# Attention and mixture-of-experts layer on one core: the input brought a second time, already turned, and normalised in that layout on GpSimd

## The reference, cut to what matters

```
x = L0_attn_x                                        # (8, 1024, 256), float32
xn = layernorm(x)                                    # (x - mean) / sqrt(var + 1e-5) over the 256 columns
q, k, v = xn @ Wq.T, xn @ Wk.T, xn @ Wv.T            # 16 heads of 16 columns
a = causal_softmax(q k^T / 4) v                      # for each of 8 sequences and 16 heads
x = x + layernorm(a @ Wo.T)
x = x + layernorm(top-2-of-8 expert FFN of layernorm(x))   # 8192 tokens, 256 -> 2 x 512 -> 256
```

## Time and profile before

| | |
|---|---|
| runs | 1973.35 us median of 3 (1972.48 to 1975.88) |
| the profiled execution | 1972.61 us, of which the profile's span is 1970.9 us |
| start | up to about 96 us (first exponentials) |
| attention | about 96 to 1150 us, a quad every 29.43 to 35.44 us |
| expert FFN and end | about 1150 to 1971 us |
| busy over the span | PE 1843.2 us (94%), DVE 1541.8 (78%), ACT 1310.9 (67%), POOL 865.1 (44%) |
| the four transposes of a pair, pairs 6 to 31 | 104 of 273 ns, line 1441 |
| normalisation on ACT, copy out of ps_w on ACT | 2 x 595 ns and 592 ns a pair |

### The profile page before, as it was taken

One profiled execution on the slowest core, in us unless ns is written; L12 is line 12 of the kernel. 1 busy time (PEld: TensorE's weight loads), 2 busy tenths in 40 slices (PEclk: granted clock), 3 DMA queues, 4 the chain that ended last, 5 costly groups with the idle time before them and its releaser, 6 DMA issues.

```text
span 1970.9 us, 75491 instructions
## 1 busy us (share of the span) xinstructions
PE 1843.2 (94%) x26766; PEld 1280.2 (65%) x26767; DVE 1541.8 (78%) x5221; ACT 1310.9 (67%) x3291; POOL 865.1 (44%) x1247
## 2 busy tenths in 40 slices
PE   6899999999999999999999899999999999999980
PEld 3245555555545555455444369999999999999970
DVE  3888888888888888888888658778777777777767
ACT  5177788888888888888787766554445445554437
POOL 4333343445545555555454744544333333333336
PEclk9799999999999999999999999999999999999995
DMA  7744657475655656465557569889899999998848
GB/s 203 219 120 131 196 171 213 150 208 183 184 172 170 189 154 203 137 192 158 167 163 234 169 206 279 240 250 265 252 260 264 257 264 261 264 262 245 239 119 342
DMA packets 255062, 411.72 MB, mean 209 GB/s; under 512 B 34480, under 2 KB 191920, under 8 KB 247600
## 3 DMA queue, kind: packets, MB, share of 16 engines
q1 hardware_dynamic: 217856, 363.46, 57.7%
q0 software_dynamic: 27120, 35.40, 10.2%
q10 hardware_dynamic: 9792, 8.93, 1.5%
HBM read 284.83 MB, written 122.28 MB: 207 GB/s over the span
## 4 chain that ended last, share of the span: by engine, by line
PE 84%; DVE 6%; ACT 4%; issue 3%; DMA 2%; SPq 1%; POOL 0%; DVEq 0%; ACTq 0%; POOLq 0%
PE ps_s L1544 18%; PE ps_s L1375 12%; PE ps_o L1428 12%; PE ps_e L1375 11%; PE ps_w L1375 11%; PE ps_e L1544 6%; PE ps_e L1561 6%; PE ps_o L1561 6%; DVE cmax L792 2%; ACT space L1275 2%; PE ps_e L1554 1%; ACT arena L1167 1%; DVE space L128 1%; PE ps_w L1504 1%; PE ps_w L1441 1%
## 5 line engine op out<-in xcount | busy, mean ns | idle before, releaser
L1167 ACT ACTIVATE arena<-ps_e 128x512 f32<-128x512 f32 (+3 forms) x1536 | 675.5, 498 | 191.8 <-PE ps_e L1375 179.0
L789 DVE CUSTOM_DVE_ANT_0 arena<-ps_s,c 128x384 bf16<-128x384 f32 (+3 forms) x1024 | 461.7, 485 | 117.2 <-PE ps_s L1375 113.5
L1375 PE MATMUL ps_e<-arena 98*32 98x512 bf16 (+3 forms) x6144 | 505.2, 327 | 28.2 <-ACT arena L1167 27.3
L1375 PE MATMUL ps_s<-arena 96*32 96x512 bf16 (+3 forms) x6144 | 509.0, 333 | 10.7 <-DVE rmax L789 3.7
L792 DVE TENSOR_REDUCE cmax<-ps_s 128x1 f32<-128x512 f32 x512 | 322.5, 680 | 28.9 <-PE ps_s L1375 28.1
L1375 PEld LDWEIGHTS ps_s<-arena 96*32 96x32 bf16 x6144 | 177.8, 96 | 211.7 <-DVE rmax L789 80.8
L1428 PE MATMUL ps_o<-arena 128*32 128x512 f32 (+3 forms) x3072 | 296.3, 486 | 6.1 <-ACT ot L1181 3.2
L1375 PEld LDWEIGHTS ps_e<-arena 98*32 98x32 bf16 x6144 | 177.7, 96 | 178.8 <-issue 82.0
L669 POOL DMA_INDIRECT acc<-blank,place_now x135 | 213.3, 1580 | 140.6 <-POOL place_now L662 66.1
L1544 PE MATMUL ps_s<-arena 128*128 128x128 f32 x2192 | 268.5, 276 | 0.8 <-ACT arena L1314 0.7
L1544 PEld LDWEIGHTS ps_s<-arena 128*128 128x128 f32 x2192 | 261.4, 192 | 8.4 <-issue 3.2
(11 more groups left out here) (182 smaller groups left out, 2714.5 us busy)
## 6 DMA issues: line engine op xcount, KB each, us to landing
arena<-in_gate_up SPq DMA_DIRECT2D x91, 1024.0 KB, 6.0
arena<-qk_parts SPq DMA_DIRECT2D x384, 128.0 KB
c_h<-in_gate_up SPq DMA_DIRECT2D x44, 1024.0 KB
qk_parts<-space SPq DMA_DIRECT2D x120, 192.0 KB, 4.4
d_xin<-xs SPq DMA_DIRECT2D x136, 130.5 KB, 3.4
arena<-v_aug SPq DMA_DIRECT2D x32, 512.0 KB, 5.0
o_t<-ot SPq DMA_DIRECT2D x64, 256.0 KB
v_aug<-space SPq DMA_DIRECT2D x28, 512.0 KB, 5.6
```

The source lines that it names most:

```text
L789: dve.tensor_tensor_reduce(summed[:, m % RJ, 0:w], ps_s[:, m % RS, 0:w], after[:, HALF - w:HALF], 1.0, LOWEST, ALU.add, ALU.max, rmax[:, p ...
L1167: act.activation(pw[:, at % RP, begin:end], ps_e[:, n % RE, 0:w], ACT.Exp, scale=SCALE).then_inc(e_done, 1)
L1375: last = pe.matmul(out[at:at + QUAD], lhsT[:, at:at + QUAD], rhs, start=start, stop=stop)
```

## The change

The host passes x a second time, transposed to 256 rows of 8192 tokens (`x_turned`). For pairs 6 to 31 it goes this way: GpSimd makes 1/sqrt and shift as before, side by side in one tile (`a_norm`); SP stores them to DRAM as two rows of 256 (`norms`), brings the turned pair into `xn_t`, waits for the store, and loads the two rows into all 128 partitions (`norm_rows`, where `xn` lay); GpSimd multiplies and adds, in place, two instructions on 128 x 512. ACT's normalisation, TensorE's four transposes and ACT's copy are left out for these pairs. q and k, with their three parts, move one slot earlier (`Q_AT`); v stays. SP's load of the next pair waits for DVE's moments instead of ACT's normalisation. GpSimd's third setting of `ks` now stands behind the scaling of pair 6. A few unused semaphores and a tile go.

```diff
+    FIRST_EVEN = 6
+    Q_AT = [start if a < FIRST_EVEN else start - 1 for a, start in enumerate(A_AT)]
...
+        norm_rows = space[:, 2560:3072].rearrange("p (z t) -> p z t", z=2)
...
+        a_norm = sb("a_norm", [P, 2, 2, 2])
+        a_rstd, a_shift = a_norm[:, :, 0], a_norm[:, :, 1]
...
+        turned_v = x_turned.rearrange("(k p) (a t) -> a p k t", p=P, t=WIDE)
+        norms_v = norms.rearrange("a z (c p) -> a p (z c)", p=P)
...  SP
-                        sp.wait_ge(a_xn, a - 1 if a < EARLY else a + 1)
+                        if a < FIRST_EVEN:
+                            sp.wait_ge(a_xn, a - 1 if a < EARLY else a + 1)
+                        else:
+                            sp.wait_ge(a_st, a + 1)
                         sp.dma_start(ax[:, a % 2], x_v[a + 2]).then_inc(ax_in[a % 2], 16)
+                for a in due(A_AT, -12, g):
+                    if a >= FIRST_EVEN:
+                        sp.wait_ge(a_shifted, a + 1)
+                        sp.dma_start(norms_v[a], a_norm[:, a % 2].rearrange("p z c -> p (z c)"), allow_slow_non_contiguous=True).then_inc(norms_out, 16)
+                for a in due(A_AT, -10, g):
+                    if a >= FIRST_EVEN:
+                        u = a % 2
+                        sp.wait_ge(a_v, a - 1)
+                        sp.wait_ge(a_xt, a)
+                        sp.dma_start(xn_t[:, u], turned_v[a]).then_inc(turned_in, 16)
+                        sp.wait_ge(norms_out, (a - FIRST_EVEN) * 16 + 16)
+                        if a == FIRST_EVEN:
+                            sp.wait_ge(a_tps, FIRST_EVEN)
+                        sp.dma_start(norm_rows, norms[a:a + 1].broadcast_to([P, 2, WIDE])).then_inc(turned_in, 16)
...  GpSimd
-                for u, (at, done_by, n) in enumerate(((BEGIN - 2, a_p3, 2 * EARLY + 2), (BEGIN + 6, a_p3, 2 * EARLY + 4), (BEGIN + 9, a_p3, 2 * EARLY + 4))):
+                for u, (at, done_by, n) in enumerate(((BEGIN - 2, a_p3, 2 * EARLY + 2), (BEGIN + 6, a_p3, 2 * EARLY + 4), (BEGIN + 9, a_xt, FIRST_EVEN + 1))):
...
+                for a in due(A_AT, -7, g):
+                    if a >= FIRST_EVEN:
+                        u, mine = a % 2, xn_t[:, a % 2]
+                        pool.wait_ge(turned_in, (a - FIRST_EVEN) * 32 + 32)
+                        pool.tensor_tensor(mine, mine, norm_rows[:, 0:1].broadcast_to([P, KT, WIDE]), ALU.mult).then_inc(a_scaled, 1)
+                        pool.wait_ge(a_scaled, a - FIRST_EVEN + 1)
+                        pool.tensor_tensor(mine, mine, norm_rows[:, 1:2].broadcast_to([P, KT, WIDE]), ALU.add).then_inc(a_xt, 1)
...
-                for a in due(A_AT, 6, g):
+                for a in due(Q_AT, 6, g):
                     third(a, 1)
-                for a in due(A_AT, 3, g):
+                for a in due(Q_AT, 3, g):
                     third(a, 0)
...  DVE: remainder(a, 0) and (a, 1) from A_AT to Q_AT
...  ACT
-                        for a in due(A_AT, 0, g):
+                        for a in due(A_AT[0:FIRST_EVEN], 0, g):
                             act.wait_ge(a_tps, a + 1)
...  first_part and second_part from A_AT to Q_AT
-                        for a in pairs_due(-2, -10, g):
+                        for a in due(A_AT[0:FIRST_EVEN], -2, g):
...  TensorE
-                        for a in due(A_AT, 0, g):
+                        for a in due(A_AT[0:FIRST_EVEN], 0, g):
                             turn_over(a)
...  the four steps of q_or_k from A_AT to Q_AT
```

More of the change, by code:

```diff
@@ L153, in combine_stage, with attention_layer @@
     return on_sync, on_gpsimd, on_scalar, on_vector
-def attention_layer(nc, x, wq_t, wk_t, wv_t, wo_t, router_t, router_bias, qk_parts, v_aug, o_t, rden, x1, xs, acc, consts, ident_b, after,
+def attention_layer(nc, x, x_turned, wq_t, wk_t, wv_t, wo_t, router_t, router_bias, qk_parts, v_aug, o_t, rden, norms, x1, xs, acc, consts, ident_b, after,
                     constants_in, kept, expert_weights, w_dn_in, biases_in, gate_up, arena, x1_all, x1_in, load_x1, out):
@@ L367, in attention_layer @@
         v_out = [sem(f"v_out{u}") for u in range(2)]
+        turned_in, norms_out, a_scaled = sem("turned_in"), sem("norms_out"), sem("a_scaled")
         c_weights_in = sem("c_weights_in")
@@ L379, in attention_layer @@
         scattered = [sem(f"scattered{u}") for u in range(2)]
-        base_set, sel_set, zero_at_ready, zeros_out, chain, tables = (sem("g_" + n) for n in ("base_set", "sel_set", "zero_at", "zeros", "chain", "tables"))
+        base_set, zero_at_ready, zeros_out, chain, tables = (sem("g_" + n) for n in ("base_set", "zero_at", "zeros", "chain", "tables"))
         x_in = [sem(f"d_x_in{s}") for s in range(RX)]
@@ L698, in _ @@
                     pool.wait_ge(a_agg, a + 1)
-                    if a >= 2:
+                    if a >= FIRST_EVEN + 2:
+                        pool.wait_ge(norms_out, (a - FIRST_EVEN - 1) * 16)
+                    elif a >= 2:
                         pool.wait_ge(a_xn, a - 1)
@@ L770, in _ @@
             for sel in sels.values():
-                dve.memset(sel[:], 0.0).then_inc(sel_set, 1)
+                dve.memset(sel[:], 0.0).then_inc(base_set, 1)
             for e in range(E):
@@ L1091, in _ @@
                             place(n, 0)
-                        for a in due(A_AT, 2, g):
+                        for a in due(Q_AT, 2, g):
                             remainder(a, 0)
-                        for a in due(A_AT, 4, g):
+                        for a in due(Q_AT, 4, g):
                             remainder(a, 1)
@@ L1242, in _ @@
                     if s == 2:
-                        for a in due(A_AT, 0, g):
+                        for a in due(A_AT[0:FIRST_EVEN], 0, g):
                             act.wait_ge(a_tps, a + 1)
-                            if a >= EARLY + 2:
-                                act.wait_ge(a_v, a - 1)
                             bank = ps_e[:, 0] if a < EARLY else ps_w[:]
                             act.activation(xn_t_of(a), bank.rearrange("p (k t) -> p k t", k=KT), ACT.Copy).then_inc(a_xt, 1)
-                        for a in due(A_AT, 2, g):
+                        for a in due(Q_AT, 2, g):
                             first_part(a, 0)
-                        for a in due(A_AT, 3, g):
+                        for a in due(Q_AT, 3, g):
                             second_part(a, 0)
-                        for a in due(A_AT, 4, g):
+                        for a in due(Q_AT, 4, g):
                             first_part(a, 1)
-                        for a in due(A_AT, 5, g):
+                        for a in due(Q_AT, 5, g):
                             second_part(a, 1)
@@ L1581, in _ @@
                             rank(n)
-                        for a in due(A_AT, 4, g):
+                        for a in due(Q_AT, 4, g):
                             q_or_k(a, 1, (1,))
                     if s == 1:
-                        for a in due(A_AT, 0, g):
+                        for a in due(A_AT[0:FIRST_EVEN], 0, g):
                             turn_over(a)
-                        for a in due(A_AT, 1, g):
+                        for a in due(Q_AT, 1, g):
                             q_or_k(a, 0, (0, 1))
-                        for a in due(A_AT, 2, g):
+                        for a in due(Q_AT, 2, g):
                             q_or_k(a, 0, (2, 3))
-                        for a in due(A_AT, 4, g):
+                        for a in due(Q_AT, 4, g):
                             q_or_k(a, 1, (2, 3))
@@ L1662, in ffn_attention_kernel @@
     o_t = scratch("o_t", [B * H // 4, P, S])
+    norms = scratch("norms", [T // 256, 2, 256])
     rden = scratch("rden", [T // 256, H, 256])
@@ L1695, in load_x1 @@
             engine.dma_start(x1_sb[:, bass.ds(n, 1)], x1_v[:, bass.ds(n, 1)]).then_inc(x1_in, 16)
-        attention_layer(nc, x, wq_t, wk_t, wv_t, wo_t, router_t, router_bias, qk_parts, v_aug, o_t, rden, x1, xs, acc, consts,
+        attention_layer(nc, x, x_turned, wq_t, wk_t, wv_t, wo_t, router_t, router_bias, qk_parts, v_aug, o_t, rden, norms, x1, xs, acc, consts,
                         consts["ident_b"], c16[:, 3 * P:3 * P + HALF], (const32, const16, c32, c16, consts_in), (base[:], table, minus_e),
@@ L1737 @@
     arrays = {
-        "x": L0_attn_x, "wq_t": by_head(L0_attn_Wq), "wk_t": by_head(L0_attn_Wk),
+        "x": L0_attn_x, "x_turned": np.asarray(L0_attn_x).reshape(T, D).T, "wq_t": by_head(L0_attn_Wq), "wk_t": by_head(L0_attn_Wk),
         "wv_t": np.asarray(L0_attn_Wv).T, "wo_t": np.asarray(L0_attn_Wo).T,
```

10 lines of the change are left out of this document (2 added, 8 removed).

## The result

The kernel after takes 2145.62 us (2137.36 to 2152.18, 4 runs), the one before 1973.19 us in the same series; the ratio is 1.0864, 95% interval 1.0843 to 1.0886. The direction was as forecast, the size was not: +172 us against +23. The profiled execution of after took 2137.36 us, its span 2135.7, which is 164.8 more than before.

A forecast was written before the change was run, and what follows sets the result against it. TensorE was taken to set the attention's pace, with one hole a quad waiting for ACT. 1972.61 + 8.9 (steady part) + 14.0 (start) = 1995.5, on the median 1996 us, slower by 1.2%; range 1974 to 2009.

The forecast's parts named there:

- SP gets three issues and a wait for the store. ... Zero: Steady part, SP's queue: the added store, loads and wait are covered by the slots between them, so they cost zero.
- The price of a packet, 0.084 us: Mean packet time of SP's queue, used to price the store of 512 single values at 2.7 us, inside the 11.
- the rows come late in every quad: Rival, chance 0.09: the store takes over some 14 us, GpSimd holds cuts, each us more costs 25; 3 us make 2071.
- The moved q and k: Steady part, slots 9 to 0: two new holes, 1.07 and 1.02 us a pair, outweigh the savings; +8.9 us in all.
- Quads with C: Quads where side work C puts the normalisation of y on ACT in slot 9: +0.41 us each, about 34.1 us.
- The start: GpSimd waits for pair 6's rows, delaying quad 0's maxima and TensorE: 15.1 us, net +14 after four saved transposes.
- the start is clear: Rival, chance 0.07: SP or the loads are some 14 us earlier at the start, the new holes stay; 1982 us.
- If nothing came back ... 41 us: Steady part: transposes off TensorE in 25 pairs save 14.8 us, 24 old holes save 26.2, if no new waits arise.
- the gain is kept: Rival, chance 0.09: slots 9 to 0 bring no new holes, so the -41 us stays; 1946 us, or 1931.
- The old hole of 1.09 us: Slot 10 before the change: TensorE waits for ACT, where a first part and the next pair's normalisation stand together; 24 quads.
- GpSimd's passes at zero: Slot 1, steady part: two added instructions of 1.28 us fit GpSimd's 2.34 us of idle time, so cost zero.
- the neutral rival: Steady part, chance 0.15: DVE is the nearer bound, time off TensorE is worth nothing, holes and savings cancel; 1987 us.

## Why the prediction was wrong

**The failed step: "SP gets three issues and a wait for the store. ... Zero".** Its price was 149 us: 2145.62 with packed values, 1996.90 with pieces of 16 bytes, nothing else different. The store itself makes 104.9 to 108.6 of it, SP's wait 28.2 to some 40; the span between the two is the 11.9 us by which the run without a store, with rows from the input, differs from the one with pieces of 16 bytes (2008.79 - 1996.90). 6.5 us of the 149 lie in the start (104.20 - 97.67). The step asked who waits for the store and whether its landing is covered. It did not ask what the store does to those who do not wait for it. The price of a packet, 0.084 us, was a mean over SP's queue, in which no store of packed single values occurs. The store's own packets came out ten times shorter, 0.008 us. What the runs show beside them is packets of other queues that took up to 8.2 us, and TensorE standing still for 66 us with no semaphore named; for neither the sum had a term.

**The rival "the rows come late in every quad"** named the store as the risk, but with another mechanism: GpSimd would hold the cuts. It never waited for the rows in the steady part. The rule cited there (the Trainium skill, DMA: Bandwidth & Descriptors, Rules for kernel authors) agrees with the trace in the count: SP's queue has 242,400 packets against 232,416 with pieces of 16 bytes, and 9984 = 26 x (512 - 128). The count is not what costs, as the values 8 bytes apart show.

**The moved q and k: right.** +8.9 us forecast, or 7.8 with the transposes of pair 6, which lie between the same two marks; the version with pieces of 16 bytes takes 1038.39 us between them where before takes 1028.29, +10.1. That its total meets the forecast within 1 us is in part luck: by the marks both parts came out longer, 16.0 and 10.1 where 15.1 and 7.8 were forecast. Quads with C forecast at 34.1 took 34.17. Without C the forecast was 0.19 shorter than before; they went from 31.87 to 31.68. The 0.05 us for the semaphore in slot 0 had no row; in the chain above DVE ends at 482.18 and TensorE starts at 482.24.

**The start: right in every step, short in one.** 15.1 us forecast; 16.0 with pieces of 16 bytes (97.67 - 81.64), 22.6 with packed ones, where SP's issue of the store took 2.98 us and that of the turned load 5.51, in place of 0.8 each (2.20 and 0.60 with pieces of 16 bytes). With the queue changed it vanished: 1980.91, where the rival "the start is clear" had 1982.

**"If nothing came back ... 41 us": wrong, though not in the sum.** It was the price of the rival "the gain is kept", 1946 us. With q and k in their old slots 1965.80 was measured. The old hole of 1.09 us is worth 0.40 (33.65 - 33.25), because ps_w, and the blocks behind it, are late the other 0.7 us. The forecast itself was spared: with the move, that late ps_w does not arise. Each new wait was asked what is late next; the one that left was not.

**GpSimd's passes at zero: right.** Two of 1.26 us a pair, and the quads came out at the forecast without them. **DVE as the nearer bound** (the neutral rival): against it, quads with C fell to 32.75 us when the holes went, with TensorE busy 32.68 of it; DVE was at 28.50.

What stays open: why packed values take so long to store, how they hold up packets of other queues, and what exactly TensorE lacks in most standstills. At 775 us it was the program; from 608 to 614 us no program transfer is recorded.

## What to carry to other kernels

When a change adds a transfer of a shape that the trace does not hold, price what it does to every other transfer and to the engines' program, not only to those who wait for it; the cheapest look is the old kernel with that one transfer added. Turn single values into rows on an engine before a store (0.20 us on DVE here) rather than letting the DMA scatter them. And a hole is worth only the distance to the next thing that is late at the same point: 0.40 of 1.09 us here.

## What the runs showed of the hardware that was not expected

- Behind stores of 2 KB in 512 packed single values, packets of other queues that had started took up to 8.2 us, and TensorE, DVE, ACT and GpSimd stopped; with the same values 8 bytes apart no packet of GpSimd's scatters took over 1.9 us, and no measurable time was lost.
- The longest wait for that store grew from 1.3 us (512 bytes apart) to 10.6 (packed), while pieces of 16 bytes, packed, took 0.6. The Trainium skill, DMA: Bandwidth & Descriptors, Specifications, says that pieces under 512 bytes are read, modified and written back; these runs show no loss from 16-byte pieces, so size alone does not tell the price.
- A program transfer of 16 KB, 1.0 us undisturbed, took 7.9 us, and TensorE stopped inside a block of four matmuls until 0.19 us after its end.
- After a standstill TensorE ran at 0.50 of its clock for some us; over the 413 us from 487 to 900 the mean granted was 0.94 against 1.00 before.
- The runs whose rows came from two separate lines of the input are some 10 us slower than the one with pieces of 16 bytes (2005 to 2009 against 1997). In the one without a store GpSimd waits 21 times, 25.7 us in all, for the reciprocals (line 733). Why was not followed up.
